# Group norms of a two-grid convolution kernel: a shorter scalar chain, and the entry in another order

## The reference

```python
def _gn(v, G=8, eps=1e-05):
    g = v.reshape(B_, G, C_ // G, H_, W_)
    m = jnp.mean(g, axis=(2, 3, 4), keepdims=True)
    s = jnp.var(g, axis=(2, 3, 4), keepdims=True)
    return ((g - m) / jnp.sqrt(s + eps)).reshape(v.shape)
...
x = x + _L0_conv_ref(_gn(x), L0_conv_W, L0_conv_b)
x = x + _L1_conv_ref(_gn(x), L1_conv_K)
x = x + _L2_conv_ref(_gn(x))
x = x + _L3_conv_ref(_gn(x), L3_conv_W, L3_conv_b)
```

## Time and profile before

| | us |
|---|---|
| median of 3 runs | 425.08 |
| the three runs | 419.27, 425.08, 427.02 |
| profiled execution, its own time | 421.93 |
| its span, first to last instruction | 420.1 |

### The profile page before, as it was taken

One profiled execution on the slowest core, in us unless ns is written; L12 is line 12 of the kernel. 1 busy time (PEld: TensorE's weight loads), 2 busy tenths in 40 slices (PEclk: granted clock), 3 DMA queues, 4 the chain that ended last, 5 costly groups with the idle time before them and its releaser, 6 DMA issues.

```text
span 420.1 us, 12385 instructions
## 1 busy us (share of the span) xinstructions
PE 391.5 (93%) x5149; PEld 197.4 (47%) x5149; DVE 291.6 (69%) x547; ACT 191.8 (46%) x299; POOL 198.6 (47%) x368
## 2 busy tenths in 40 slices
PE   8999999999998999796988899999989999999773
PEld 5444454444544555342444455464444544544341
DVE  4788797464945469948698788796365855459854
ACT  7653345444407357644202345353545324347543
POOL 6177785565676344300000376683766685442400
PEclk9999999999999999978999999999999999999899
DMA  6076678978788757610000165677978787551601
GB/s 236 8 219 140 141 163 198 217 146 189 157 153 150 170 127 162 117 37 2 1 2 2 29 189 131 143 152 182 212 154 170 148 173 141 114 106 34 114 2 51
DMA packets 26280, 52.32 MB, mean 125 GB/s; under 512 B 11120, under 2 KB 12784, under 8 KB 26224
## 3 DMA queue, kind: packets, MB, share of 16 engines
q1 hardware_dynamic: 13904, 29.65, 31.7%
q0 software_dynamic: 12032, 21.15, 24.0%
q10 hardware_dynamic: 288, 0.72, 0.4%
HBM read 12.22 MB, written 0.52 MB: 30 GB/s over the span
## 4 chain that ended last, share of the span: by engine, by line
POOL 27%; PE 25%; DMA 22%; DVE 12%; issue 6%; ACT 5%; SPq 2%; DVEq 0%; ACTq 0%
DMA inp<-cell_out 21%; POOL inp L555 19%; PE bank L575 14%; PE bank L624 10%; POOL shifts L545 7%; ACT act_out L814 3%; DVE cell_out L1038 3%; DVE inp L1001 2%; SPq L514 2%; DVE inp L745 2%; DMA raw<-weights_in 1%; DVE inp L752 1%; ACT inp L745 1%; DVE cell_out L1032 1%; DVE stat L888 1%
## 5 line engine op out<-in xcount | busy, mean ns | idle before, releaser
L555 POOL DMA_DIRECT2D inp<-cell_out x304 | 162.2, 542 | 131.2 <-DVE cell_out L1038 129.6
L575 PE MATMUL bank<-inp,w_heavy 128*32 128x512 f16 (+1 forms) x1536 | 140.5, 384 | 4.1 <-DMA inp<-cell_out 1.9
L814 ACT ACTIVATE act_out<-bank,bias 128x512 f32<-128x512 f32 x152 | 98.9, 688 | 84.5 <-PE bank L624 55.6
L1038 DVE TENSOR_TENSOR cell_out<-act_out,cell_out 128x512 f16<-128x512 f32 x148 | 102.3, 695 | 49.1 <-ACT act_out L814 45.4
L575 PE MATMUL bank<-inp,w_light 96*32 96x512 f16 (+2 forms) x1440 | 120.8, 404 | 11.1 <-DVE inp L1001 6.1
L575 PEld LDWEIGHTS bank<-inp,w_heavy 128*32 128x32 f16 (+1 forms) x1536 | 64.1, 102 | 71.5 <-issue 14.6
L575 PEld LDWEIGHTS bank<-inp,w_light 96*32 96x32 f16 (+2 forms) x1440 | 59.9, 105 | 70.6 <-issue 16.7
L808 ACT ACTIVATE cell_out<-bank,bias 128x512 f16<-128x512 f32 x56 | 39.0, 696 | 95.9 <-PE bank L575 65.6
L624 PE MATMUL bank<-cell_out,w_first 32*128 32x512 f16 (+1 forms) x1296 | 61.4, 378 | 0.3 <-DVE cell_out L1032 0.3
L545 POOL DMA_DIRECT2D shifts<-inp x48 | 29.8, 627 | 62.5 <-DMA inp<-cell_out 51.3
L1032 DVE CAST cell_out<-act_out 128x512 f16<-128x512 f32 x92 | 39.2, 426 | 15.1 <-ACT act_out L814 14.7
(11 more groups left out here) (53 smaller groups left out, 166.8 us busy)
## 6 DMA issues: line engine op xcount, KB each, us to landing
inp<-cell_out SPq DMA_DIRECT2D x104, 72.2 KB, 3.6
inp<-cell_out SPq DMA_DIRECT2D x104, 71.2 KB, 3.9
raw<-weights_in SPq DMA_DIRECT2D x8, 672.0 KB, 5.3
inp<-cell_out POOLq DMA_DIRECT2D x112, 36.1 KB, 2.9
inp<-cell_out POOLq DMA_DIRECT2D x112, 35.1 KB, 3.0
raw<-weights_in SPq DMA_DIRECT2D x6, 576.0 KB, 5.1
inp<-cell_out POOLq DMA_DIRECT2D x40, 72.2 KB, 4.5
inp<-cell_out POOLq DMA_DIRECT2D x40, 71.2 KB, 5.0
```

Source lines behind the costliest of these rows:

```text
L555: pool.dma_start(to, source).then_inc(signal, 16)
L575: last = pe.matmul(bank[j % BANKS][p:p + m, :], home[i][0:rows, w:w + m], source[:, off:off + PAIRS, dx:dx + SIDE], start=n == 0, stop=n = ...
L814: act.activation(act_out[:, n % T_RING, :], bank[j % BANKS][:, :], ACT.Relu, bias=bias[:, col + part[k]:col + part[k] + 1], scale=1.0 / W_ ...
L1038: dve.tensor_tensor(low, t, high, ALU.subtract).then_inc(cell_written, 1)
```

## The change

The arithmetic of the norms changes, and so does the order of the entry.

- `averager` in the first product is replaced by `deviator`, the identity less `averager`: PE gives the offset itself. DVE squares it straight from PE's bank (`share`), and computes the mean behind that, where the copy was.
- `square_root` gets a second ACT instruction, `spread` = -(variance + eps)/16. DVE's four steps become three: `inverse` = 1/root, `ratio` = inverse * inverse * spread, `scale` = (ratio + 0.75) * inverse. The second reciprocal is gone.
- The constants are one matrix larger, and come in three transfers: the deviator and the row mask, then the averager, both on ACT's queue ahead of the weights; the partner matrix on SP's, behind the biases. POOL has one more memset of one column.
- In the entry ACT takes half 0's root ahead of the weights' high part. DVE finishes half 0's high part before it turns to half 1's statistics, and PE's products for half 1's norm lie inside half 0's convolution (after steps 2 and 8). The borders of half 1's rows 2 and 3 are zeroed behind the first cell's output.
- In the middle, norm 3 of half 0 is written in float32 by ACT (`full_part`) instead of by DVE, and DVE does the low part of it behind `tokens`.

```diff
-        const = sb("const", [128, 257], F32)
-        averager, partner, row_mask = const[:, 0:128], const[:, 128:256], const[:, 256:257]
+        const = sb("const", [128, 385], F32)
+        deviator, row_mask, averager, partner = const[:, 0:128], const[:, 128:129], const[:, 129:257], const[:, 257:385]
...
@@ SP
             sp.dma_start(bias[:, :], biases).then_inc(biases_loaded, 16)
+            sp.dma_start(const[:, 257:385], consts[:, 257:385]).then_inc(consts_loaded, 16)
...
@@ POOL
             pool.memset(eps4[:, :], 0.25 * GN_EPS)
+            pool.memset(eps16[:, :], -0.0625 * GN_EPS)
...
@@ PE
-                pe.matmul(bank[j % BANKS][:, 0:1], averager, data, start=True, stop=True).then_inc(sums_ready, 1)
+                pe.matmul(bank[j % BANKS][:, 0:1], deviator if st[0] == "mean" else averager, data, start=True, stop=True).then_inc(sums_ready, 1)
...
-            pe.wait_ge(consts_loaded, 16)
+            pe.wait_ge(deviator_loaded, 16)
             group_mean(0, 0)
             keep_busy(BANKS - 1, 2)
+            pe.wait_ge(averager_loaded, 16)
             group_var(0, 0)
-            keep_busy(BANKS - 1, 2)
+            conv_in_place(cells[0], 3)
             group_mean(0, 1)
-            conv_in_place(cells[0], 14)
+            conv_in_place(cells[0], 9)
             group_var(0, 1)
             conv_in_place(cells[0])
...
@@ ACT
                 act.activation(root[:, b:b + 1], bank[j % BANKS][:, 0:1], ACT.Sqrt, bias=eps4[:, 0:1],
                                scale=0.25).then_inc(root_ready[b], 1)
+                act.activation(spread[:, b:b + 1], bank[j % BANKS][:, 0:1], ACT.Identity, bias=eps16[:, 0:1],
+                               scale=-0.0625).then_inc(spread_ready[b], 1)
...
+            def full_part(b):
+                act.activation(normed[:, b, :], res[:, b, :], ACT.Identity, bias=centre[:, b:b + 1],
+                               scale=scale[:, b:b + 1]).then_inc(normed_ready, 1)
...
-            act.dma_start(const[:, :], consts).then_inc(consts_loaded, 16)
+            act.dma_start(const[:, 0:129], consts[:, 0:129]).then_inc(deviator_loaded, 16)
+            act.dma_start(const[:, 129:257], consts[:, 129:257]).then_inc(averager_loaded, 16)
...
-            for r in range(2):
+            for r in range(3):
                 zero_pads(0, r)
+            square_root(0, 0)
             weights_high(0)
-            square_root(0, 0)
...
             square_root(2, 1)
+            full_part(0)
             evacuate(cells[2 * N_GRID])
...
@@ DVE, group_var
-                step(dve.tensor_tensor(offset[:, own_column], own[:, b, 0:1], bank[j % BANKS][:, 0:1], ALU.subtract))
-                dve.scalar_tensor_tensor(share[:, own_column], offset[:, own_column], offset[:, own_column],
+                dve.scalar_tensor_tensor(share[:, own_column], bank[j % BANKS][:, 0:1], bank[j % BANKS][:, 0:1],
                                          own[:, b, 1:2], ALU.mult, ALU.add).then_inc(stat_ready[b], 1)
-                dve.tensor_copy(mean[:, own_column], bank[j % BANKS][:, 0:1]).then_inc(dve_bank_read[b], 1)
+                dve.tensor_tensor(mean[:, own_column], own[:, b, 0:1], bank[j % BANKS][:, 0:1],
+                                  ALU.subtract).then_inc(dve_bank_read[b], 1)
...
@@ DVE, group_scale
                 step(dve.reciprocal(inverse[:, column], root[:, column]))
-                dve.tensor_scalar(ratio[:, column], bank[j % BANKS][:, 0:1], GN_EPS, inverse[:, column],
-                                  ALU.add, ALU.mult).then_inc(dve_bank_read[b], 1)
+                dve.wait_ge(spread_ready[b], n + 1)
+                dve.scalar_tensor_tensor(ratio[:, column], inverse[:, column], inverse[:, column],
+                                         spread[:, column], ALU.mult, ALU.mult).then_inc(dve_bank_read[b], 1)
                 dve.wait_ge(dve_bank_read[b], emptied[j][1])
-                step(dve.scalar_tensor_tensor(better[:, column], ratio[:, column], 0.25, root[:, column],
-                                              ALU.mult, ALU.add))
-                step(dve.reciprocal(scale[:, column], better[:, column]))
+                step(dve.scalar_tensor_tensor(scale[:, column], ratio[:, column], 0.75, inverse[:, column],
+                                              ALU.add, ALU.mult))
```

More of the change, by code:

```diff
@@ L274, in build @@
         bias = sb("bias", [128, 8 * COLS * ROWS], F32)
-        const = sb("const", [128, 257], F32)
-        averager, partner, row_mask = const[:, 0:128], const[:, 128:256], const[:, 256:257]
+        const = sb("const", [128, 385], F32)
+        deviator, row_mask, averager, partner = const[:, 0:128], const[:, 128:129], const[:, 129:257], const[:, 257:385]
         stat6 = sb("stat6", [128, HALVES, 6], F32)
         own = sb("own", [128, HALVES, 2], F32)
-        mean, offset, share, ratio, root, inverse, better, scale = (
+        mean, share, spread, ratio, root, inverse, scale = (
             sb(name, [128, HALVES], F32) for name in
-            ("mean", "offset", "share", "ratio", "root", "inverse", "better", "scale"))
+            ("mean", "share", "spread", "ratio", "root", "inverse", "scale"))
         centre = sb("centre", [128, HALVES], F32)
         eps4 = sb("eps4", [128, 1], F32)
+        eps16 = sb("eps16", [128, 1], F32)
         rowsum = sb("rowsum", [128, HALVES, SIDE], F32)
@@ L309, in build @@
         root_ready = [sem(f"root_ready{b}") for b in range(HALVES)]
+        spread_ready = [sem(f"spread_ready{b}") for b in range(HALVES)]
         rowsum_ready = [sem(f"rowsum_ready{b}") for b in range(HALVES)]
@@ L830, in _ @@
             act.activation(warm[:, :], zeros[:, 0:1], ACT.Sqrt)
-            for r in range(2):
+            for r in range(3):
                 zero_pads(0, r)
+            square_root(0, 0)
             weights_high(0)
-            square_root(0, 0)
-            for r in range(2, ROWS):
-                zero_pads(0, r)
-            for r in range(ROWS):
-                last = zero_pads(1, r)
+            for r in range(3, ROWS):
+                last = zero_pads(0, r)
             last.then_inc(pads_zeroed, 1)
+            zero_pads(1, 0)
+            zero_pads(1, 1)
             square_root(0, 1)
@@ L842, in _ @@
             act.wait_ge(biases_loaded, 16)
-            for st in cells[:2 * N_GRID - 1]:
+            grid_cell(cells[0])
+            for r in range(2, ROWS):
+                last = zero_pads(1, r)
+            last.then_inc(pads_zeroed, 1)
+            for st in cells[1:2 * N_GRID - 1]:
                 grid_cell(st)
@@ L936, in normalise, with high_first @@
                                          ALU.subtract, ALU.mult)
[L938 removed]
+            def high_first(b):
                 step(normalise(b))
@@ L944, in enter @@
                 dve.tensor_copy(high, t).then_inc(high_split, 1)
-                if meanwhile is not None:
-                    weights_low(meanwhile)
-                low_part(n, b)
             def conv_add(st):
@@ L1099, in _ @@
             group_var(2, 1)
-            step(normalise(0))
             row_sums(1)
-            low_part(3, 0)
             group_scale(2, 1)
-            token_sums(1)
+            token_sums(1, meanwhile=0)
             gates(1)
```

32 lines of the change are left out of this document (21 added, 11 removed).

## The result

| | before | after |
|---|---|---|
| executions (timed beside each other) | 4 | 4 |
| median, us | 422.56 | 429.17 |
| lowest and highest, us | 419.27, 427.02 | 426.00, 433.26 |
| profiled execution, its own time, us | 421.93 | 433.26 |
| its span, us | 420.1 | 431.5 |

The ratio is 1.0157, with a 95% interval of 1.009 to 1.0223: slower, where I had forecast 0.4% faster.

What follows compares the result with a forecast made beforehand. PE was busy 93% of the span, but POOL's issuing and DMAs made half the chain, inside the unchanged grids. Entry 0.24 plus middle 1.28 gave 1.5 us off 423.5, forecast 422.0 us, range 416.5 to 426.5.

Steps and rivals of the forecast that it cites:

- slower rival: A shifted PE pause puts the clock at half: 3.6 us lost, 1.5 won, 425.6 us; chance 0.20.
- (a): Entry: `offset` goes, so PE's variance product can start at 5.74 instead of 5.92 us, ending at 6.33.
- (b): Entry: the root no longer queues behind the weights and starts at 6.37 us; ACT's being free just fits.
- (c): Entry, root to `normalise`: 0.86 instead of 1.12 us, 0.26 less; `normalise` at 7.23, PE's start at 8.39.
- (d): Entry: weights' load, issued 0.44 us later, allows their high part at 6.65; it ends 0.5 us before DVE is done.
- weights land after 7.2 us and hold the start: Entry: a stated condition under which the prediction is wrong; the load was expected to give 6.62 us.
- (e): Entry: half 1's mean product now stands between convolution steps and gives back 0.35 us.
- (f): First convolution: PE's clock step stays at 10.4 us, giving back 0.58; an earlier step wins up to 0.43 more.
- The middle: Between the grids: gain 1.28 us, bounds 0.7 and 1.5, from earlier variance, shorter norms and PE's vanished wait for `tokens`.
- Whatever is won there moves the rest of the program forward as a block: Entry and middle gains reach the end whole, since the grids' transfers and waits all follow from them.
- Nothing in the change lengthens a pause: PE's pauses: the argument against the slower rival, adding that the change can shorten such a loss as well.
- The range: Whole kernel, single executions' spread included: 416.5 us (fastest run less largest gain) to 426.5 (slowest rival's 425.6 and a little).

Runs made afterwards that it cites:

- before_again: The kernel before, unchanged, run against itself with a second profile: ratio 1.0003 (0.9951 to 1.0056), mean 424.6 us.
- after_again: The changed kernel, unchanged, run once more against the kernel before: ratio 1.0060 (0.9990 to 1.0130), mean 425.9 us.
- before_filled: The kernel before with 12 zero products instead of 8 at the entry and 24 instead of 8 in the middle: ratio 0.9925, mean 422.5 us.
- before_gap: The kernel before without the 8 zero products ahead of half 0's convolution: ratio 1.0078 to the kernel before, mean 427.4 us.
- arith: The kernel before with the norms' new arithmetic alone, constants of 385 columns in one transfer: ratio 0.9919 to the kernel before, mean 424.4 us.
- consts3: The kernel before with only its constants changed, 385 columns in three transfers: ratio 1.0014 to the kernel before, mean 425.4 us.

## Why the prediction was wrong

It forecast 422.0 and gave the slower rival 0.20 at 425.6; measured were 429.2, and 426.8 over 16 executions. Its prices for the start and the middle were near, and what it said of all the rest was not. By its steps:

- **(a) and (b) held, (c) gave less.** The root came at 6.33 (6.37 forecast), `spread` behind it at 6.50, `normalise` at 7.35 instead of 7.23. From root to there it took 1.02 us, where I had 0.86 and the old chain 1.12, so the shorter scale saved 0.10 at the entry and not 0.26.
- **(d) failed.** I let the load of the weights last 5.00 us behind an issue 0.44 later, with ACT ready at 6.62. It took 5.83 and landed at 7.49, so the weights and not the norm set the start: 8.73, not 8.39. This is the condition "weights land after 7.2 us and hold the start". The start lost 0.34 of the 1.17, of which 0.12 are the norm's.
- **(e) held**: the mean product takes 9.81 - 9.50 = 0.31 us (0.35).
- **(f) had the wrong question.** I asked when the clock rises in the convolution. It rose at 5.8 us in this trace, and at 3.9 to 16.6 in the twenty; the first cell's outputs then start between 15.6 and 20.2. I had quoted the Trainium skill that the number of slow matmuls at a start changes from run to run, and then built the likeliest case on one draw all the same. Of the 0.58 that the sum gives back this trace shows nothing, since the clock was up ahead of the convolution. I also never asked what an early rise does to PE's cover ahead of the convolution.
- **The middle** was undersized: the distance from the L1 convolution, forecast to shrink from 32.48 to 31.5, shrank to 30.81, by 1.67 us instead of 1.0.
- **The step that failed** is in the first paragraph: "Whatever is won there moves the rest of the program forward as a block". In the first pair of profiles the start and the middle together came 1.24 us earlier, a fall of the clock in the middle included, and behind and between them L0 was 3.0 and L3 9.6 us longer. Over all profiles the grid L0 differs by 1.9 ± 1.1 us, L3 by 0.7 ± 1.2, while the start is 1.4 ± 0.5 and the stretch around the middle 1.8 ± 0.6 us shorter. And the grids are no fixed block: in the eight profiles with the old arithmetic L0 took 166.7 to 174.4 us and L3 158.3 to 164.3, and each of these ranges is wider than the whole gain. Why the grids were longer in the changed kernel is open.
- **"Nothing in the change lengthens a pause"**, in the slower rival, failed too, by less than it seems. The entry's pause went from 0.16 to 1.53 us between the two first profiles, but at like clocks the change adds 0.2 to 0.3 us. The middle's kept its 1.85, and behind it the clock fell in six of nine profiles, where it never did with the old arithmetic; why there is not shown. I had named a pause of 2.12 to 2.50 us as the dangerous size and taken the ones of 0.16 and 1.86 for harmless. Filling the entry's pause took 3 to 4 us off the changed kernel and 2 off the one before, so the pauses carry time, but the profiles show at most 1.5 to 2.1 us of it, and not that the change made the kernel slower by them.
- **The range** reached one mechanism's 425.6 and little more. Single executions of the kernel before spread over 4%, so a median of four can lie 2 us from its mean, and did: 429.2 against 426.8.

What stays open. The grid L0 is 171.9 us in the mean of the twelve profiles with the new arithmetic and 170.0 in the eight with the old. A part of it, 0.43 us, is the same in all of them (below). The rest could be scatter, and much of the scatter lies at one place, where PE waits for a cell output to land, here in before_again:

```profile
138.59 2.77 PE L575 MATMUL bank<-inp,w_heavy 128*64 128x512 f16 x12 [3.50 <-DMA inp<-cell_out]
```

This wait was 1.13 us in the first profile of the same kernel, 3.98 in after_again, 6.02 in before_filled. In nine of the twenty profiles, three of them with the old arithmetic, the clock fell at 137 to 146 us, near the end of this wait, and L0 is 173.0 us there, against 169.6 in the other eleven. What makes the landing late was not tested. L3's 9.6 us in the first profile did not come back: the other eight profiles of the changed kernel and its variants have 160.4 to 164.2 there, as before has (158.3 to 164.3). And the falls that a trace shows are worth about half of what covering the pauses gave.

## What to carry to other kernels

Filler that keeps PE busy over a wait is part of the schedule: when an edit moves either end of the wait, size the filler anew, and size it for the fast clock, where it lasts half as long. The price is a later start at the slow clock, where twelve products last 2.7 us instead of 1.5. Do not take the parts that an edit leaves alone for a block of fixed length: read how much they vary between profiles of one kernel before adding a gain in front of them to the end. After an edit that shortens a chain, look in PE's windows for granted clocks under 1.00 behind its pauses before judging the edit. Where single executions spread over 4%, four of them don't tell 0.5% from 1.5%: run the two unchanged kernels again before explaining their difference.

## What the runs showed of the hardware

**The clock fell behind shorter pauses than I thought of**: to half behind 1.50 us (after_again, 8.7 to 12.1 us), 1.85 us (the middle) and 2.15 us (before_gap, 7.9 to 14.7). In arith it fell at 7.5 us, early in the eight zero products, and since its first instruction PE had had no pause longer than this one:

```profile
5.41 0.35 PE L646 MATMUL bank<-own,const 128*128 128x1 f32 x2 [0.90 <-DVE own L898]
```

In turn there was no fall behind 1.53 us (after) and 1.27 (before_again) at the entry, nor in three profiles behind the same 1.85 us in the middle, so the length of a pause alone does not decide. The Trainium skill ("TensorE: Matmul & The Clock Gate") advises against pauses above some 3 us ("Why this matters for your kernels"), and Part 1 tells of a kernel whose clock went up and down with frequent short pauses between its groups of matmuls; the falls named above came without any pause of 3 us, which is nearer to the second case. Those in L0, at 137 to 146 us, stand by waits of 2.0 to 6.0 us.

**The load of the weights varied by more than the added transfers explain.** From issue to landing its 576 KB took 5.0 to 5.6 us in the eleven profiles with the constants in one transfer, and 4.8 to 5.8 us in the eight with two transfers ahead of it on ACT's queue. The 5.83 of the first profile is at the upper end of these. What each of the eight has is the later issue, by 0.48 us.

**A stall of DVE at a fixed place.** From the fifth cell's outputs of L0 to the sixth's it is 2.33 to 2.34 us in the eight profiles with the old arithmetic and 2.74 to 2.81 in the twelve with the new, nothing between. DVE's first cast there, before and then after:

```profile
35.25 0.43 DVE L1032 CAST cell_out<-act_out 128x512 f16<-128x512 f32 x1 [0.93 <-ACT act_out L814]
```

```profile
34.83 0.43 DVE L1053 CAST cell_out<-act_out 128x512 f16<-128x512 f32 x1 [1.35 <-ACT act_out L829]
```

ACT's outputs had begun at 34.44 and 33.59, so the cast starts 0.81 and 1.24 us behind them, with the same wait in the code. A fetch of DVE's code, moved by its different number of instructions, is a guess that no run tests: a packet of the instruction queue q14 lies near the cast in after (35.2 us), but also in consts3 (39.4 us, with the cast at 38.80), which has no stall.
